# Time mix base rows loaded half a batch early into the sum's own tiles, modulation rows stored in two steps, gate floors on 128 partitions

## Chip, cores and metric

The kernel runs as one program on one core of a Trainium2 chip. The time is the device time of one execution in microseconds (us). The engines are named as in the profile: PE (TensorE), PEld (its weight loads), DVE (VectorE), ACT (ScalarE), POOL (GpSimd), SP (SyncE, which here only issues DMAs).

## What is computed

One AdaLN block on x of 4 batches x 512 tokens x 512 channels in float32. A small conditioning matrix c (4 x 512) gives six modulation rows per batch, `mod = (silu(c) @ wmod).reshape(4, 6, 1, 512)`: sa, ca, ga, sb, cb, gb. Two of them, ga and gb, are floored in size: `(2 * (g >= 0) - 1) * max(|g|, 0.25)`. Then:

```
h  = layernorm(x) * (1 + ca) + sa                       # h0 in the kernel
x2 = h + (sigmoid(r) * wkv) @ Wo.T                      # time mix; r, k, v from layernorm(h) and its shift by one token
x3 = x2 + sigmoid(...) * (silu(... @ Wkey.T) @ Wval.T)  # channel mix, from layernorm(x2)
x4 = x + ga * x3
h5 = layernorm(x4) * (1 + cb) + sb
out = x4 + gb * (shared experts(h5) + top-2 of 16 routed experts(h5))
```

The change touches four places: where h is added to the output projection of the time mix (x2), where the six modulation rows go to memory, where ga and gb are floored, and the element type of a small table of integers that the routed experts read.

## The kernel before, in words

The kernel is written by hand with one instruction stream for each engine, in a fixed order, and semaphores between them. Every float32 product is three matmuls of split operands (high x high, high x low, low x high; `mm3`, L423 to L427). There are three stages: the time mix (about the first 300 us), the channel mix (to about 690 us) and the experts.

**Time mix.** It runs over four batches b = 0 to 3, each of four tiles j of 128 tokens. For each batch PE computes K, V and R (48 matmuls each), turns the next batch's normalized rows over (L880), and then computes O, the output projection (48 matmuls, 12 for each tile), into the four banks `mm_ps[0]` to `mm_ps[3]`. The next user of bank j is K of the next batch. PE may start it only when DVE has read bank j (`bank_free`, which waits on `s_x2` after an O).

DVE reads the banks of O in `o_out(b, j)` (L1377 to L1386): `x2b[:, j] = mm_ps[j] + h0r[:, t % 2]`, where t = 4b + j. `h0r` is a ring of two tiles, into which SP loads the rows of h (`h0_s`) from memory (`load_h0`, L604 to L610). `h0_s` was stored by SP earlier (`store_h0`) from the tiles `xb`, because `xb` is overwritten with the next batch. The four calls of `o_out(b, .)` stand among the work on K and V of batch b + 1 in DVE's order (L1509 to L1533). Behind them come statistics of x2, and then first_norm_a to first_norm_d of batch b + 2 (L1446 to L1456), whose result is waited for by ACT, PE and POOL in turn: `centred(2, b)` gives ACT what it needs for `hn_out(2, b)`, and PE turns that over (`turn(2, b, ...)`) between V tile 1 and V tile 2 of batch b + 1, and between V tile 2 and V tile 3.

**SP's order in batch 0** (L638 to L673): store h of batch 0; store modulation rows 0 and 1; load the first norm's rows and x of batch 1; load four half weights (`load_tm` 4 to 7); wait for all six modulation rows (`s_modsb` at 7) and for the floors of ga and gb (`s_ke` at 3); store modulation rows 2 to 5; store h of batch 1; load half weights 8 and 9; wait until the six rows are in memory; load `h0r` for tiles 0 and 1; then the rows and x of batch 2; then, tile by tile, store x2 and load `h0r` for tile 2, and again for tile 3.

**Modulation rows.** ACT copies each row set (4 batches x 512) from PSUM to `modr` (4 partitions x 6 slots x 512; `rows_out`, L2086). The tile `modr` lies on the same memory as `h0r` (slots 0 and 1) and `x2b` (slots 2 to 5), so nothing may be loaded into these before the rows are stored. The rows come in the order 0, 1, 2, 5, 3, 4 (`row_order`, L401). DVE floors row 2 (ga) in `gate_floor(2)` at L1427, ahead of the first batch's differences, and row 5 (gb) in `gate_floor(5)` at L1501, between r_out and rw_lo of batch 0; each is four instructions on 4 partitions x 512. ga and gb are read from memory for the first time after the time mix.

**Table of words.** `tab` (1 x 2 x 52, int32) is written once by DVE (L1838). PE reads one word of it for each 128-row tile of the routed experts (`word_of`, L1178) and waits on a semaphore against it (`up`, L1189); SP reads two for each tile (`tile_of`, L818). There are 41 such tiles in this run.

Of the kernel before, what the change touches and what calls it, by code (L numbers as in the profile page):

```python
# [14 lines left out]
BF16 = mybir.dt.bfloat16  # L15
I32 = mybir.dt.int32
ALU = mybir.AluOpType
ACT = mybir.ActivationFunctionType
# [47 lines left out]
def adaln_block(nc, x_d, c_d, wmod_d, vecs_d, wtm_d, wcm_d, wrt_d, wex_d, out_d):  # L66
    top = ExitStack()
    with top:
# [27 lines left out]
        pos = sbuf(top, "pos", [P, 2, NT], I32)  # L96
        tab = sbuf(top, "tab", [1, 2, NSX], I32)
        tend = sbuf(top, "tend", [1, NE + 3], I32)
# [28 lines left out]
        overlay.close()  # L127
        h0r = sbuf(ph1, "h0r", [P, 2, H])
        x2b = sbuf(ph1, "x2b", [P, TT, H])
# [14 lines left out]
        sgc = sbuf(ph1, "sgc", [P, KT, NB])  # L144
        overlay = ExitStack()
        modt = sbuf(overlay, "modt", [NB, 2, H])
        overlay.close()
        srb = sbuf(ph1, "srb", [P, 2, H])
# [168 lines left out]
        s_srst = [sem("s_srst0"), sem("s_srst1")]  # L317
        s_h0r = [sem("s_h0r0"), sem("s_h0r1")]
        s_x2 = sem("s_x2")
# [80 lines left out]

        row_order = [0, 1, 2, 5, 3, 4]  # L401

        order1 = []
# [135 lines left out]
        def xk_in(b, k):  # L539

            n = b * KT + k
            if b:
                return xkr[:, n % 2], s_xkr[n % 2], 16 * (n // 2)
            if k < 2:
                return xkr[:, k], s_xkr[k], 16
            return raw[:, k - 2], s_h0r[k - 2], 16 * (NT // 2 + 1)

# [8 lines left out]
        def _(sp):  # L556
# [46 lines left out]

            def load_h0(b, tiles):  # L604
                for j in tiles:
                    t = b * TT + j
                    sp.wait_ge(s_h0st[j], 16 * (b + 1))
                    if t >= 2:
                        sp.wait_ge(s_x2, t - 1)
                    sp.dma_start(h0r[:, t % 2], h0_s[t]).then_inc(s_h0r[t % 2], 16)  # L610

# [27 lines left out]
            sp.wait_ge(s_modsb, 3)  # L639
            for i in (0, 1):  # L640
                sp.dma_start(mod_s[i], modr[:, i]).then_inc(s_modst, 16)
            load_bc(1)
            load_x(1)
            for n in (4, 5, 6, 7):
                load_tm(n)
            sp.wait_ge(s_modsb, 7)
            sp.wait_ge(s_ke, 3)
            for i in range(2, 6):
                sp.dma_start(mod_s[i], modr[:, i]).then_inc(s_modst, 16)
            for b in range(NB):  # L650
                if b + 1 < NB:
                    store_h0(b + 1)
                if b == 0:
                    load_tm(8)
                    load_tm(9)
                    sp.wait_ge(s_modst, 16 * 6)
                load_h0(b, [0, 1])
                if b + 2 < NB:
                    load_bc(b + 2)
                if b:  # L660
                    store_xk(b - 1)
                if b + 2 < NB:
                    load_x(b + 2)
                if b == NB - 1:
                    load_half(10, cm_half(10))
                    load_half(11, cm_half(11))
                if b:
                    store_sr(b - 1, [0] if b == NB - 1 else range(TT))
                store_x2(b, [0])
                load_h0(b, [2])  # L670
                store_x2(b, [1])
                load_h0(b, [3])
                store_x2(b, [2, 3])  # L673
            load_half(12, cm_half(12))
# [21 lines left out]
            sp.wait_ge(s_mm, mm_count("S", NB - 1, 3))  # L696
            sp.wait_ge(s_modst, 16 * 6)

# [559 lines left out]
        def _(dve):  # L1258
# [118 lines left out]
            def o_out(b, j):  # L1377
                if b == 0 and j == 0:
                    dve.wait_ge(s_modst, 16 * 6)
                t = b * TT + j  # L1380
                dve.wait_ge(s_mm, mm_count("O", b, j))
                dve.wait_ge(s_h0r[t % 2], 16 * (t // 2 + 1))
                if b:
                    dve.wait_ge(s_x2st[j], 16 * b)
                    dve.wait_ge(s_hn, hn_count(2, b - 1, j))
                dve.tensor_tensor(x2b[:, j], mm_ps[j][:, :], h0r[:, t % 2], ALU.add).then_inc(s_x2, 1)  # L1386

# [21 lines left out]

            def gate_floor(i):  # L1410

                src = modr[:, i]
                dve.wait_ge(s_modsb, row_count(i))
                done(dve.tensor_scalar(modt[:, 0], src, 0.0, 2.0, ALU.is_ge, ALU.mult))
                done(dve.tensor_scalar(modt[:, 1], src, -1.0, 0.25, ALU.mult, ALU.max))
                done(dve.tensor_tensor(modt[:, 1], src, modt[:, 1], ALU.max))
                dve.scalar_tensor_tensor(out=src, in0=modt[:, 0], scalar=-1.0, in1=modt[:, 1],
                                         op0=ALU.add, op1=ALU.mult).then_inc(s_ke, 1)
# [7 lines left out]
            dve.tensor_scalar(floor[:, :], vecs[:, V_FIRST, :], -1.0, PP0, ALU.mult, ALU.add).then_inc(s_ke, 1)  # L1426
            gate_floor(2)  # L1427
            differences(1, 0, [0, 1])
# [15 lines left out]
            for b in range(NB):  # L1444
# [34 lines left out]
                if b:  # L1479
                    mixed_lo("S", b - 1, 0)  # L1480
                    mixed("S", b - 1, 2)
                    mixed_lo("S", b - 1, 1)
                    mixed("X", b - 1, 0)
                    mixed("S", b - 1, 3)
                    mixed_lo("S", b - 1, 2)
                    r_out(b, 0)
                    mixed("X", b - 1, 1)
                    mixed_lo("S", b - 1, 3)
                    r_out(b, 1)
                    rw_lo(b, 0)  # L1490
                    mixed("X", b - 1, 2)
                    mixed("X", b - 1, 3)
                    r_out(b, 2)
                    rw_lo(b, 1)
                    r_out(b, 3)
                    rw_lo(b, 2)
                    rw_lo(b, 3)
                else:
                    r_out(b, 0)
                    r_out(b, 1)  # L1500
                    gate_floor(5)  # L1501
                    rw_lo(b, 0)
                    r_out(b, 2)
                    rw_lo(b, 1)
                    r_out(b, 3)
                    rw_lo(b, 2)
                    rw_lo(b, 3)
# [487 lines left out]
        def _(act):  # L1995
# [80 lines left out]
            def sr_out(b, tiles=range(TT)):  # L2076
                for j in tiles:
                    t = b * TT + j
                    act.wait_ge(s_mm, mm_count("S", b, j))
                    if t >= 2:  # L2080
                        act.wait_ge(s_srst[t % 2], 16 * (t // 2))
                    else:
                        act.wait_ge(s_ke, 3)
                    act.activation(srb[:, t % 2], mm_ps[j][:, :], ACT.Sigmoid).then_inc(s_sr, 1)

            def rows_out(i, bank):  # L2086

                act.wait_ge(s_modps, rows_summed(i))
                if i in (1, 4):
                    ins = act.activation(modr[:, i], bank[0:NB, :], ACT.Identity, bias=1.0)  # L2090
                else:
                    ins = act.activation(modr[:, i], bank[0:NB, :], ACT.Copy)
                ins.then_inc(s_modsb, 1)
# [530 lines left out]
```

## Time and profile before

| | |
|---|---|
| time, median of 3 runs | 942.76 us (938.45, 942.76, 944.33) |
| span of the profiled execution | 937.6 us from its first to its last instruction |
| busy share of the span | PE 95%, PEld 77%, DVE 56%, ACT 41%, POOL 41% |
| mean granted PE clock | 0.984 of full speed |
| chain of work that ended last | PE 71%, DVE 12%, DMA 5%, issue 4%, ACT 3%, POOL 3% |

The page gives no time of the profiled execution beside its span; the fastest of the three runs is 0.85 us above that span and the slowest 6.7 us. Times in the views count from the span's start. An engine's idle time is put down to what ended it ("<-"). Busy spans of PE overlap, as matmuls are pipelined: at full clock one 128x512 matmul starts 0.23 us after the one before and is shown as 0.39 us long.

### The profile page before, as it was taken

The numbers are of one execution on the slowest core, as the hardware profiler recorded it, in microseconds if no ns is written. First come the engines' busy times: TensorE is split into PE (matmuls) and PEld (weight loads), VectorE is DVE, ScalarE is ACT, GpSimd is POOL, SyncE is SP. The second block draws the span as 40 slices with busy tenths as digits, with TensorE's granted clock in tenths as the row PEclk, the third lists the DMA queues.
The fourth block names the chain that finished last, engine by engine and source line by source line (L and its number), as shares of the span: only waits on it lengthen the run. The fifth ranks groups of instructions, "written<-read, shape, count | busy, mean of one in ns | idle before, by whom it ended". The sixth has DMA issues, their size and how long they took to land.

```text
span 937.6 us, 13563 instructions
## 1 busy us (share of the span) xinstructions
PE 892.2 (95%) x4264; PEld 719.0 (77%) x4265; DVE 529.4 (56%) x999; ACT 383.2 (41%) x632; POOL 381.2 (41%) x282
## 2 busy tenths in 40 slices
PE   7899869999998999999999999999999999999996
PEld 2457658878776888788888888888877888888875
DVE  5897797988667111274327432742486444444488
ACT  2557565573736533322232223215452333333352
POOL 2332200100022446416301630167815599998573
PEclk9899989999998999999999999999999999999999
DMA  9548578566046426876212521267353789876887
GB/s 357 192 129 255 199 231 256 158 203 203 23 157 209 144 97 206 243 239 209 91 34 72 198 90 34 87 203 282 114 157 124 247 248 278 279 247 223 260 252 194
DMA packets 121824, 174.03 MB, mean 186 GB/s; under 512 B 8216, under 2 KB 69656, under 8 KB 118704
## 3 DMA queue, kind: packets, MB, share of 16 engines
q1 hardware_dynamic: 58896, 111.55, 34.9%
q0 software_dynamic: 9216, 34.61, 12.1%
q10 hardware_dynamic: 53664, 27.26, 9.9%
q8 instruction: 27, 0.44, 0.2%
q14 instruction: 21, 0.17, 0.1%
HBM read 97.58 MB, written 75.81 MB: 185 GB/s over the span
## 4 chain that ended last, share of the span: by engine, by line
PE 71%; DVE 12%; DMA 5%; issue 4%; ACT 3%; POOL 3%; SPq 1%; DVEq 0%; ACTq 0%
PE kk_ps L425 6%; PE kk_ps L427 6%; PE kk_ps L426 6%; PE kv_ps L425 6%; PE kv_ps L427 6%; PE kv_ps L426 6%; PE mm_ps L425 4%; PE mm_ps L426 4%; PE mm_ps L427 4%; PE up_ps L425 3%; PE dn_ps L425 3%; PE dn_ps L427 3%; PE dn_ps L426 3%; PE up_ps L426 2%; PE up_ps L427 2%
## 5 line engine op out<-in xcount | busy, mean ns | idle before, releaser
L1563 DVE TENSOR_TENSOR silu<-kk_ps,silu 128x512 fp32r<-128x512 f32 x64 | 44.2, 691 | 196.5 <-ACT silu L2229 196.2
L2225 ACT ACTIVATE kk_ps<-kk_ps 128x512 f32<-128x512 f32 x64 | 37.2, 582 | 206.5 <-PE kk_ps L427 206.5
L425 PE MATMUL kk_ps<-xk,cm_w 128*128 128x512 f32 x256 | 100.9, 394 | 2.3 <-DVE xk L1608 2.3
L425 PE MATMUL kv_ps<-cm_w,silu 128*128 128x512 f32 x256 | 100.6, 393 | 0.0
L427 PE MATMUL kk_ps<-xk,cm_w 128*128 128x512 f32 x256 | 99.8, 390 | 0.0
L427 PE MATMUL kv_ps<-cm_w,silu 128*128 128x512 f32 x256 | 99.7, 390 | 0.0
L426 PE MATMUL kk_ps<-xk,cm_w 128*128 128x512 f32 x256 | 99.6, 389 | 0.0
L426 PE MATMUL kv_ps<-cm_w,silu 128*128 128x512 f32 x256 | 99.6, 389 | 0.0
L2393 POOL TENSOR_TENSOR cm_w<-stage,cm_w 128x1024 fp32r<-128x1024 f32 x16 | 38.7, 2423 | 90.5 <-ACT cm_w L2013 74.7
L2400 POOL TENSOR_TENSOR rs<-mv,neghalf 128x4 f32<-128x4 f32 (+2 forms) x13 | 13.8, 1065 | 144.1 <-DVE mv L1274 144.0
L1890 DVE TENSOR_TENSOR xsT<-xs_ps,xsT 128x512 fp32r<-128x512 f32 x42 | 28.9, 691 | 73.9 <-ACT xsT L2310 73.9
L2449 POOL TENSOR_TENSOR rs<-mv,neghalf 128x1 f32<-128x1 f32 x16 | 16.1, 1008 | 126.9 <-DVE mv L1588 126.9
L2041 ACT ACTIVATE mix<-raw_ps 128x512 fp32r<-128x512 f32 x64 | 37.6, 596 | 66.8 <-DVE raw_ps L1345 63.5
L425 PE MATMUL mm_ps<-mix,wkv_w 128*128 128x512 f32 x128 | 54.0, 422 | 8.8 <-DVE x2b L1386 4.6
L425 PEld LDWEIGHTS kk_ps<-xk,cm_w 128*128 128x128 f32 x256 | 48.1, 188 | 12.1 <-ACT xk L2221 2.6
L427 PEld LDWEIGHTS kk_ps<-xk,cm_w 128*128 128x128 f32 x256 | 48.1, 188 | 10.3
L427 PEld LDWEIGHTS kv_ps<-cm_w,silu 128*128 128x128 f32 x256 | 48.0, 188 | 10.3
L426 PEld LDWEIGHTS kv_ps<-cm_w,silu 128*128 128x128 f32 x256 | 48.1, 188 | 9.8
L426 PEld LDWEIGHTS kk_ps<-xk,cm_w 128*128 128x128 f32 x256 | 48.1, 188 | 9.7
L425 PEld LDWEIGHTS kv_ps<-cm_w,silu 128*128 128x128 f32 x256 | 48.1, 188 | 9.6
L426 PE MATMUL mm_ps<-mix,wkv_w 128*128 128x512 f32 x128 | 52.3, 409 | 0.0
L2442 POOL DMA_INDIRECT xs_s<-stage,pos x32 | 31.5, 985 | 50.9 <-DVE pos L1682 42.4
(297 smaller groups left out, 2361.6 us busy)
## 6 DMA issues: line engine op xcount, KB each, us to landing
xs_s<-zero ACTq DMA_DIRECT2D x13, 1024.0 KB, 6.1
ys_s<-zero ACTq DMA_DIRECT2D x13, 1024.0 KB, 6.3
xsb<-xs_s SPq DMA_DIRECT2D x44, 256.0 KB, 3.8
ys_s<-ysb SPq DMA_DIRECT2D x41, 256.0 KB, 3.4
ex_raw<-in_wex POOLq DMA_DIRECT2D x9, 1024.0 KB, 6.3
stage<-in_wcm SPq DMA_DIRECT2D x16, 512.0 KB, 3.7
wmod<-in_wmod SPq DMA_DIRECT2D x6, 1024.0 KB, 11.8
ex_raw<-in_wex SPq DMA_DIRECT2D x6, 1024.0 KB, 8.0
```

The costliest lines, as they stand in the source:

```text
L425: pe.matmul(out, lhs[0], rhs[0], start=first, stop=False)
L426: pe.matmul(out, lhs[0], rhs[1], start=False, stop=False)
L427: return pe.matmul(out, lhs[1], rhs[0], start=False, stop=last)
L1563: dve.tensor_tensor(silu[:, g % NSILU, 1, :], kk_ps[g % 2][:, :], silu[:, g % NSILU, 0, :].bitcast(F32), ALU.subtract).then_inc(s_silo, 1)
L1890: dve.tensor_tensor(xsT[:, par, 1], xs_ps[par][:, :, :], xsT[:, par, 0].bitcast(F32), ALU.subtract)\
L2041: act.activation(mix[:, i % 2, 0, k, :], raw_at(s, b, k), ACT.Copy)\
L2225: act.activation(kk_ps[g % 2][:, :], kk_ps[g % 2][:, :], ACT.Silu).then_inc(s_silu, 1)
L2393: pool.tensor_tensor(w[:, 1, k0:k0 + KT // 2, :], stage[:, n % 2].rearrange("p (k c) -> p k c", c=H), w[:, 0, k0:k0 + KT // 2, :].bitcast( ...
L2400: pool.tensor_tensor(rs[:, j0:j1].rearrange("p (t a) -> p t a", a=1), mv[:, j0:j1, 1:2], neghalf[:, :].rearrange("p (t a) -> p t a", a=1). ...
L2442: pool.indirect_dma_start(xs_s, bass.IndirectOffsetOnAxis(ap=pos[:, c, t:t + 1], axis=0), h5_row(t), None).then_inc(s_scat[t % TT], 16)
L2449: pool.tensor_tensor(rs5[:, t % 2:t % 2 + 1], mv5[:, t % 2, 1:2], neghalf[:, :], ALU.pow)\
```

## The change

- `load_h0` loads all four tiles of a batch at once, straight into `x2b`, early in the batch's half; `o_out` adds the bank to `x2b` in place. The waits that guard `x2b` (its last store, and ACT's last reading) move from DVE's `o_out` to SP's `load_h0`. `h0r` is gone; in its room lie `flo` and a filler.
- The modulation rows get other slots (`row_slot`), so that rows 0 to 3 lie on `x2b`, and 4 and 5 on the room of `flo`. Rows 2 and 3 are stored when row 3 is there, without a floor; rows 4 and 5 later.
- `gate_floor(2)` and `gate_floor(5)` go. In their place SP loads ga and gb back from memory, spread over 128 partitions x 16 elements each, DVE floors both together in batch 1 (four instructions on 128 x 32), and SP stores them over the rows in memory.
- `tab` has 16-bit words.

```diff
-        tab = sbuf(top, "tab", [1, 2, NSX], I32)
+        tab = sbuf(top, "tab", [1, 2, NSX], U16)
...
-        h0r = sbuf(ph1, "h0r", [P, 2, H])
+        flo = sbuf(ph1, "flo", [P, 4, 2, H // 32])
+        sbuf(ph1, "flo_rest", [P, 2 * H - 4 * H // 16])
...
         row_order = [0, 1, 2, 5, 3, 4]
+        row_slot = [2, 3, 4, 5, 1, 0]
...
-            def load_h0(b, tiles):
-                for j in tiles:
-                    t = b * TT + j
+            def load_h0(b):
+                for j in range(TT):
                     sp.wait_ge(s_h0st[j], 16 * (b + 1))
-                    if t >= 2:
-                        sp.wait_ge(s_x2, t - 1)
-                    sp.dma_start(h0r[:, t % 2], h0_s[t]).then_inc(s_h0r[t % 2], 16)
+                    if b:
+                        sp.wait_ge(s_x2st[j], 16 * b)
+                        sp.wait_ge(s_hn, hn_count(2, b - 1, j))
+                    sp.dma_start(x2b[:, j], h0_s[b * TT + j]).then_inc(s_h0r[j], 16)
+
+            def store_rows(rows):
+                for i in rows:
+                    sp.dma_start(mod_s[i], modr[:, row_slot[i]]).then_inc(s_modst, 16)
+
+            def spread(i):
+                return mod_s[i].rearrange("b (q c) -> (b q) c", c=H // 32)
...
             for n in (4, 5, 6, 7):
                 load_tm(n)
-            sp.wait_ge(s_modsb, 7)
-            sp.wait_ge(s_ke, 3)
-            for i in range(2, 6):
-                sp.dma_start(mod_s[i], modr[:, i]).then_inc(s_modst, 16)
+            sp.wait_ge(s_modsb, row_count(3))
+            store_rows([2, 3])
             for b in range(NB):
                 if b + 1 < NB:
                     store_h0(b + 1)
                 if b == 0:
+                    sp.wait_ge(s_modst, 16 * 4)
+                load_h0(b)
+                if b == 0:
+                    sp.wait_ge(s_modsb, row_count(4))
+                    store_rows([4, 5])
                     load_tm(8)
                     load_tm(9)
-                    sp.wait_ge(s_modst, 16 * 6)
-                load_h0(b, [0, 1])
                 if b + 2 < NB:
                     load_bc(b + 2)
+                if b == 0:
+                    sp.wait_ge(s_modst, 16 * 6)
+                    for n, i in enumerate((2, 5)):
+                        sp.dma_start(flo[:, 0, n], spread(i)).then_inc(s_flo, 16)
                 if b:
                     store_xk(b - 1)
...
-                store_x2(b, [0])
-                load_h0(b, [2])
-                store_x2(b, [1])
-                load_h0(b, [3])
-                store_x2(b, [2, 3])
+                store_x2(b, range(TT))
+                if b == 1:
+                    sp.wait_ge(s_ke, 2)
+                    for n, i in enumerate((2, 5)):
+                        sp.dma_start(spread(i), flo[:, 3, n]).then_inc(s_modst, 16)
...
             def o_out(b, j):
-                if b == 0 and j == 0:
-                    dve.wait_ge(s_modst, 16 * 6)
-                t = b * TT + j
                 dve.wait_ge(s_mm, mm_count("O", b, j))
-                dve.wait_ge(s_h0r[t % 2], 16 * (t // 2 + 1))
-                if b:
-                    dve.wait_ge(s_x2st[j], 16 * b)
-                    dve.wait_ge(s_hn, hn_count(2, b - 1, j))
-                dve.tensor_tensor(x2b[:, j], mm_ps[j][:, :], h0r[:, t % 2], ALU.add).then_inc(s_x2, 1)
+                dve.wait_ge(s_h0r[j], 16 * (b + 1))
+                dve.tensor_tensor(x2b[:, j], mm_ps[j][:, :], x2b[:, j], ALU.add).then_inc(s_x2, 1)
...
-            def gate_floor(i):
+            def gate_floors():
-                src = modr[:, i]
-                dve.wait_ge(s_modsb, row_count(i))
-                done(dve.tensor_scalar(modt[:, 0], src, 0.0, 2.0, ALU.is_ge, ALU.mult))
...
+                src, sign, size, out = (flo[:, i].rearrange("p a c -> p (a c)") for i in range(4))
+                dve.wait_ge(s_flo, 32)
+                done(dve.tensor_scalar(sign, src, 0.0, 2.0, ALU.is_ge, ALU.mult))
+                done(dve.tensor_scalar(size, src, -1.0, 0.25, ALU.mult, ALU.max))
+                done(dve.tensor_tensor(size, src, size, ALU.max))
+                dve.scalar_tensor_tensor(out=out, in0=sign, scalar=-1.0, in1=size,
+                                         op0=ALU.add, op1=ALU.mult).then_inc(s_ke, 1)
...
-            gate_floor(2)
...
                     rw_lo(b, 3)
+                    if b == 1:
+                        gate_floors()
                 else:
                     r_out(b, 0)
                     r_out(b, 1)
-                    gate_floor(5)
...
-                    else:
-                        act.wait_ge(s_ke, 3)
                     act.activation(srb[:, t % 2], mm_ps[j][:, :], ACT.Sigmoid).then_inc(s_sr, 1)
```

## Rows read from the trace of the kernel before

**Rows 1.** Chain that ended last, 86 to 105 us: start, length, what.

```profile
86.64 8.48 DMA h0r<-h_s
95.24 0.70 DVE x2b L1386
...
96.78 6.89 DMA h0r<-h_s
```

**Rows 2.** Waits between 85 and 130 us: engine, line, releaser, total, times, longest.

```profile
PE tp_ps L880 <- ACT hT L2031: 7.0, 1, 7.0
...
DVE x2b L1386 <- DMA h0r<-h_s: 5.0, 2, 3.5
PE mm_ps L425 <- DVE x2b L1386: 4.6, 2, 2.8
```

**Rows 3.** Timeline of DVE, 93 to 113 us: start, length, instruction, idle before.

```profile
93.08 0.68 DVE L1351 TENSOR_TENSOR mix<-raw_ps,mix 128x512 fp32r<-128x512 f32 x1
95.24 0.69 DVE L1386 TENSOR_TENSOR x2b<-mm_ps,h0r 128x512 f32<-128x512 f32 x1 [1.47 <-DMA h0r<-h_s]
...
103.77 0.69 DVE L1386 TENSOR_TENSOR x2b<-mm_ps,h0r 128x512 f32<-128x512 f32 x1 [3.52 <-DMA h0r<-h_s]
...
112.54 0.16 DVE L1320 SCALAR_TENSOR_TENSOR nm<-mv,rs 128x4 f32<-128x4 f32 x1 [0.36 <-POOL rs L2400]
```

**Rows 4.** Timeline of PE, 93 to 129 us, in the same columns.

```profile
93.73 0.39 PE L427 MATMUL mm_ps<-wro_w,rw 128*128 128x512 f32 x1
95.99 0.50 PE L425 MATMUL mm_ps<-mix,wkv_w 128*128 128x512 f32 x1 [1.86 <-DVE x2b L1386]
...
104.51 0.50 PE L425 MATMUL mm_ps<-mix,wkv_w 128*128 128x512 f32 x1 [2.75 <-DVE x2b L1386]
...
105.32 0.52 PE L425 MATMUL mm_ps<-mix,wkv_w 128*128 128x512 f32 x1
...
108.96 0.40 PE L425 MATMUL mm_ps<-mix,wkv_w 128*128 128x512 f32 x1
...
117.49 1.09 PE L880 MATMUL tp_ps<-ident,hn 128*128 128x128 f32 x8 [0.16 <-ACT hn L2023]
...
128.29 1.94 PE L880 MATMUL tp_ps<-ident,hn 128*128 128x128 f32 x8 [6.96 <-ACT hT L2031]
```

**Rows 5.** Timeline of ACT, 59 to 117 us.

```profile
59.98 0.59 ACT L2092 ACTIVATE modr<-tp_ps 4x512 f32<-4x512 f32 x1 [1.88 <-PE tp_ps L863]
...
105.16 0.60 ACT L2041 ACTIVATE mix<-raw_ps 128x512 fp32r<-128x512 f32 x1 [5.48 <-DVE raw_ps L1345]
...
115.93 1.51 ACT L2023 ACTIVATE hn<-x2b,nm,rs 128x512 f32<-128x512 f32 x2
```

**Rows 6.** Waits of SP's queue, whole span.

```profile
SPq L647 <- DVE modr L1417: 27.0, 1, 27.0
...
SPq L575 <- DMA mod_s<-modr: 2.2, 1, 2.2
```

**Rows 7.** Timeline of DVE around the second floor, 80 to 83 us.

```profile
80.21 0.68 DVE L1417 SCALAR_TENSOR_TENSOR modr<-modt 4x512 f32<-4x512 f32 x1
...
82.79 0.69 DVE L1370 TENSOR_TENSOR eT<-mm_ps,eT 128x512 f32<-128x512 f32 x1
```

**Rows 8.** Timeline of DVE, batch 1, 149 to 161 us.

```profile
149.68 2.49 DVE L1327 TENSOR_TENSOR dT<-hT 128x512 f32<-128x512 f32 x4
...
160.52 0.69 DVE L1386 TENSOR_TENSOR x2b<-mm_ps,h0r 128x512 f32<-128x512 f32 x1 [1.87 <-PE mm_ps L427]
```

**Rows 9.** Groups of DVE by line and shape: count, busy, mean ns, idle before.

```profile
L1776 DVE TENSOR_TENSOR pr<-pr 128x32 f32<-128x32 f32 x1 | 0.2, 194 | 0.0
```

**Rows 10.** Busy time by stretch: PE, PEld, DVE, ACT, POOL, granted clock, DMA share, GB/s.

```profile
105.00:109.00 4.00, 4.00 (x13) 3.10 (x12) 3.90 (x11) 3.82 (x6) 2.22 (x1) 0.57 0.46 159
...
145.00:166.00 21.00, 21.00 (x103) 17.60 (x102) 17.43 (x27) 10.95 (x18) 0.00 (x0) 1.00 0.81 253
```

**Rows 11.** Waits between 660 and 860 us, the routed experts.

```profile
PEld up_ps L425 <- issue: 7.8, 33, 0.4
```

More of the change, by code:

```diff
@@ L16 @@
 I32 = mybir.dt.int32
+U16 = mybir.dt.uint16
 ALU = mybir.AluOpType
@@ L144, in adaln_block @@
         sgc = sbuf(ph1, "sgc", [P, KT, NB])
-        overlay = ExitStack()
-        modt = sbuf(overlay, "modt", [NB, 2, H])
-        overlay.close()
         srb = sbuf(ph1, "srb", [P, 2, H])
@@ L317, in adaln_block @@
         s_srst = [sem("s_srst0"), sem("s_srst1")]
-        s_h0r = [sem("s_h0r0"), sem("s_h0r1")]
+        s_h0r = [sem(f"s_h0r{i}") for i in range(TT)]
+        s_flo = sem("s_flo")
         s_x2 = sem("s_x2")
@@ L545, in xk_in @@
                 return xkr[:, k], s_xkr[k], 16
-            return raw[:, k - 2], s_h0r[k - 2], 16 * (NT // 2 + 1)
+            return raw[:, k - 2], s_h0r[k - 2], 16 * (NB + 1)
         def bank_free(eng, s, b, j):
@@ L639, in _ @@
             sp.wait_ge(s_modsb, 3)
-            for i in (0, 1):
-                sp.dma_start(mod_s[i], modr[:, i]).then_inc(s_modst, 16)
+            store_rows([0, 1])
             load_bc(1)
@@ L645, in _ @@
                 load_tm(n)
-            sp.wait_ge(s_modsb, 7)
-            sp.wait_ge(s_ke, 3)
-            for i in range(2, 6):
-                sp.dma_start(mod_s[i], modr[:, i]).then_inc(s_modst, 16)
+            sp.wait_ge(s_modsb, row_count(3))
+            store_rows([2, 3])
             for b in range(NB):
@@ L696, in _ @@
             sp.wait_ge(s_mm, mm_count("S", NB - 1, 3))
-            sp.wait_ge(s_modst, 16 * 6)
+            sp.wait_ge(s_modst, 16 * 8)
             def load_ga(b):
@@ L1408, in centred_last @@
                                          op0=ALU.mult, op1=ALU.mult).then_inc(s_nm3, 1)
-            def gate_floor(i):
-                src = modr[:, i]
-                dve.wait_ge(s_modsb, row_count(i))
-                done(dve.tensor_scalar(modt[:, 0], src, 0.0, 2.0, ALU.is_ge, ALU.mult))
-                done(dve.tensor_scalar(modt[:, 1], src, -1.0, 0.25, ALU.mult, ALU.max))
-                done(dve.tensor_tensor(modt[:, 1], src, modt[:, 1], ALU.max))
-                dve.scalar_tensor_tensor(out=src, in0=modt[:, 0], scalar=-1.0, in1=modt[:, 1],
+            def gate_floors():
[5 more added lines that the diff above has]
+                dve.scalar_tensor_tensor(out=out, in0=sign, scalar=-1.0, in1=size,
                                          op0=ALU.add, op1=ALU.mult).then_inc(s_ke, 1)
@@ L2088, in rows_out @@
                 act.wait_ge(s_modps, rows_summed(i))
+                row = modr[:, row_slot[i]]
                 if i in (1, 4):
-                    ins = act.activation(modr[:, i], bank[0:NB, :], ACT.Identity, bias=1.0)
+                    ins = act.activation(row, bank[0:NB, :], ACT.Identity, bias=1.0)
                 else:
-                    ins = act.activation(modr[:, i], bank[0:NB, :], ACT.Copy)
+                    ins = act.activation(row, bank[0:NB, :], ACT.Copy)
                 ins.then_inc(s_modsb, 1)
```

## The prediction, on record before the result

> **What bounds the kernel.** PE is busy for 95% of the span, so I looked first for the places where it is not, and for what stands behind them. The chain of waits shows one stretch in which a transfer ends last: two loads into `h0r`, 8.5 and 6.9 us, one ahead of the first `o_out` of batch 0 and one ahead of the third [rows 1]. The waits of the same stretch say who pays [rows 2]: DVE stood 5.0 us for the loads, and PE 4.6 us for DVE's reading of the banks. There is a second, longer gap of PE, 7.0 us for ACT's `hT`. Whether the change is worth 4.6 or 5.0 us, or less, hangs on what leads to that second gap.
>
> On DVE [rows 3] the work before the first `o_out` starts at 93.08 and ends at 93.76; then DVE idles 1.47 us for the first load. It idles 3.52 us for the load of tile 2 ahead of 103.77. Behind that it is all but continuous up to 112.54, where it waits 0.36 us for POOL. PE [rows 4] ends O of batch 0 at 93.73 + 0.39 = 94.12, starts K of batch 1 at 95.99, waits again ahead of 104.51, then for `hn` ahead of 117.49 (0.16 us), then for `hT` ahead of 128.29. The last two are waits for work that DVE's order leads to: statistics of x2, `hn_out`, first norm. So from 95 to 128 us DVE's order and PE's are both near the bound, and DVE's ends last at 117.49 and 128.29.
>
> **The change, part by part.**
>
> *Base rows.* The first load of `h0r` is issued at 86.64 [rows 1] because SP stands 27.0 us for all six rows and both floors [rows 6]. Afterwards SP waits only for row 3, which ACT has out at 59.98 + 0.59 = 60.6 [rows 5], and for four rows in memory: the nearest row for that wait is 2.2 us [rows 6]; doubled, 4.4 us, it still leaves SP free at 66. Four loads, with 1 us allowed for the issue of each and the longest landing, 8.5 us [rows 1], are in by 66 + 4 + 8.5 = 79 us. DVE can use them at 93.76, so there are about 15 us to spare. Both idle times go: 1.47 + 3.52 = 4.99 us on DVE. What is late next at each `o_out`? Tile 0 is then bound by DVE's own work (93.76), tile 2 too, at 103.77 - 4.99 = 98.78; its bank is ready at 94.12 at the latest.
>
> The rest of DVE's work up to 112.54 has one foreign term, POOL: it sits behind ACT's weight copies, which follow an ACT instruction that itself stood 5.48 us for DVE's `raw_ps` [rows 5]. So ACT and POOL move with DVE. The last `hn_out` (two instructions from 115.93, ending 117.44 [rows 5]) ends at 112.45.
>
> PE, seen alone, would gain more. K of batch 1 can start 0.06 us after the first `o_out`, which ends at 93.76 + 0.69 = 94.45, that is at 94.5 instead of 95.99: 1.48 us. The second gap, 2.75 us, goes, as bank 2 is read by 98.78 + 0.69 = 99.5 and PE reaches it at 94.5 + 24 x 0.23 = 100.0. And after that gap the granted clock was 0.57 for 4 us [rows 10]: nine matmul intervals took 108.96 - 105.32 = 3.64 us [rows 4] where nine of 0.2275 us take 2.05, so 1.6 us went to the lower of the two levels, 1.2 GHz. In all PE would come to its turn 1.48 + 2.75 + 1.6 = 5.8 us earlier, at 117.49 - 0.16 - 5.8 = 111.5. There it finds `hn` at 112.45 and waits 0.9 us. So the gain at this point is 4.99 us, and at the wait for `hT` too.
>
> Here a rule and the rows part. The Trainium skill (TensorE: Matmul & The Clock Gate, Part 1) says that the array runs throttled after idling and that activity releases it, which would price a removed gap at the gap and the slow stretch behind it. By that rule the sum is 5.8 us; by the rows it is 5.0, since DVE's order ends last. I take the rows.
>
> *Does it carry to the end?* From 130 us PE is busy without a break: in 145 to 166 us for 21.00 of 21.00 us [rows 10], and what follows waits on semaphores of these engines, not on a clock. No transfer of batch 1 to 3 is waited for by `o_out` (both waits for `h0r` [rows 2] lie in batch 0), so the early loads bring nothing there. They stand on SP behind two new waits, x2's last store and ACT's last reading; in batch 3, where the base loads come first in the turn, SP has then only stores queued behind. I cost that at nothing.
>
> *What SP is moved past.* Behind `load_h0` of batch 0 stand rows 4 and 5, half weights 8 and 9, the rows and x of batch 2. They come earlier than before, as the stop of 27.0 us is gone. The two loads and two stores of the floors on 128 partitions (64-byte pieces) add four issues, at the same allowance 4 us; nothing waits for their landing but DVE half a batch later. Cover: SP's idle time; without it 4 us on SP.
>
> *Floors.* The first floor ran while DVE waited for `hT`. The second ends at 80.89, its last and longest instruction 0.68 us long [rows 7], so all four take at most 2.7 us. But the last r_out at 82.79 waits for ACT's sigmoid, which stands in ACT's order behind the copies of what PE turns over, so taking that time away ahead of it moves nothing. The new floors are four instructions on 128 x 32, 0.19 us each by the nearest row [rows 9], 0.8 us with their waits, put ahead of 149.68 in batch 1 [rows 8]; DVE idles 1.87 us for PE ahead of 160.52, which hides it. Without that cover: 0.8 us.
>
> *16-bit words.* The trace shows no word load itself. The nearest row is PEld's "issue" ahead of `up` [rows 11]: 7.8 us in 33 times, 0.24 us for a tile, with the word's load and its waits in it. One word is read where one was read before, so I take 0. Bounds: the 0.24 us doubled for 41 tiles, +9.7 us; below, the 0.24 us gone, -9.7 us, which would need the load to be the whole gap and free afterwards, so I keep -1 at most for it.
>
> **Sum.** 4.99 us off, nothing added: the profiled execution's span goes from 937.6 to 932.6 us. The median of the runs shown, 942.76, stands 5.2 us above that span, the fastest 0.85 us; I carry the difference over: 942.76 - 4.99 = 937.8 us.
>
> **Rivals.**
>
> *PE's clock adds to it (0.13).* If the slow stretch behind 128.29 shrinks as well (eight turns in 1.94 us against 1.09 at 117.49 [rows 4], so 0.9 us, and about as much again in the matmuls behind it), the gain is 5.0 + 1.8 = 6.8: 936.0 us. For it: PE-bound from there. Against it: the 7 us gap ahead of it stays whole.
>
> *A new wait takes the place of the old one (0.12).* The change does then not do what it says: the base rows are still not there, or the turn finds something else late, such as the weights for S or x of batch 2. If only the first idle time goes, 942.76 - 1.47 = 941.3; if neither, 942.8. Against it: 15 us to spare, and loads behind it that are all moved forward. For it: the moved transfers meet the zero fills that ACT issues in 60 to 80 us.
>
> *The word load costs more (0.05): slower.* It is read on PE ahead of every routed tile's `up`, where PE has little slack. It decides from 4.99 / 41 = 0.12 us for each word on; at a doubled 0.24 us the time is 942.76 - 4.99 + 9.7 = 947.5. For it: PE's sequencer does stand there [rows 11]. Against it: the same instruction with a narrower operand.
>
> **Numbers.** The forecast has 0.70. Range: the runs shown spread from 938.45 to 944.33. Low end: 938.45 less 6.8 is 931.7. High end: the case of only the first wait, 941.3, with half of that spread, 1.5 to 3 us, is 943.5. I give 932 to 943.5; outside lie the word's case and single odd draws, under 0.2. A change of 1% here is 9.4 us (about what a measurement of this kernel tells from none): under 933.3 is faster, over 952.2 slower. The forecast of 0.53% lies within; the clock's case comes nearest to the one bound, the word's case reaches the other only at 0.35 us for each word. So faster 0.11, same 0.86, slower 0.03.
>
> **What would show it.** After the change DVE has no wait for a load at `o_out`, the first starts right behind the split ahead of it, and the third about 5 us after the first (8.5 before). PE's two waits for `x2b` in batch 0 shrink to some 0.4 us together, the clock stays at its upper level there, and PE waits about 1 us for `hn` ahead of the turn and still 7 us for `hT`. SP issues the base loads near 65 us. The floors show as four instructions of 0.2 us in batch 1 with PE's O unmoved. PEld's "issue" ahead of `up` stays at 0.24 us. The prediction is wrong if DVE's idle time reappears between 98 and 128 us, if batch 1's PE stretch starts less than 4.5 us earlier, or if the routed stage changes its length by more than 1 us.

## The result, and the profile after

The changed kernel takes 935.2 us (median of 9 runs), the kernel before 942.44 us (median of 9): a ratio of 0.9924, 95% interval 0.9899 to 0.9948, or 7.2 us less (4.9 to 9.5). One of the nine runs after took 1786.43 us; the ratio leaves it out. The forecast was 937.8 us and a ratio of 0.9947, just inside the interval. Two further sets of runs gave 0.9921 (0.9889 to 0.9954) and 0.9945 (0.9923 to 0.9967). The three, weighted by the inverse squares of their intervals, make 0.9933 (0.9918 to 0.9947), that is 6.3 us less (5.0 to 7.7). So there is a gain, and it is most likely a little more than the 5.0 us of the sum.

The profiled execution of the changed kernel spans 932.3 us, against 937.6. It reached batch 0's first `r_out` 0.68 us later than the one before (76.77 against 76.09). Over all 14 traces that mark lies between 75.63 and 77.20 us, and over the traces of each of the two orders it spreads by 0.75 us or more, so positions below are also given from it.

SP's timeline after, 61 to 85 us (start, length, instruction), answers to [rows 6] and to the loads of [rows 1]:

```profile
61.34 0.61 SPq L615 DMA_DIRECT2D mod_s<-modr  x2
61.98 1.80 SPq L603 DMA_DIRECT2D h_s<-xb  x4
63.88 2.22 SPq L611 DMA_DIRECT2D x2b<-h_s  x4
...
82.36 2.44 SPq L570 DMA_DIRECT2D xb<-in_x  x4
```

The stop of 27.0 us is gone, the four base loads are issued from 63.88, and batch 2's x, which left SP at 90.05 before, leaves at 82.36. DVE's timeline after, for [rows 3]:

```profile
93.83 0.68 DVE L1363 TENSOR_TENSOR mix<-raw_ps,mix 128x512 fp32r<-128x512 f32 x1
94.43 0.68 DVE L1392 TENSOR_TENSOR x2b<-mm_ps,x2b 128x512 f32<-128x512 f32 x1
...
99.34 0.67 DVE L1392 TENSOR_TENSOR x2b<-mm_ps,x2b 128x512 f32<-128x512 f32 x1
...
108.12 0.16 DVE L1332 SCALAR_TENSOR_TENSOR nm<-mv,rs 128x4 f32<-128x4 f32 x1 [0.35 <-POOL rs L2405]
```

Neither sum has an idle time in front of it. The first starts right behind the split; the third comes 4.91 us after the first, 8.53 before. POOL's 0.35 us stays. PE after, for [rows 4], with the restart in batch 2 as a last row:

```profile
95.17 0.50 PE L426 MATMUL mm_ps<-mix,wkv_w 128*128 128x512 f32 x1 [0.28 <-DVE x2b L1392]
...
113.06 1.09 PE L892 MATMUL tp_ps<-ident,hn 128*128 128x128 f32 x8 [1.27 <-ACT hn L2029]
...
123.88 1.94 PE L892 MATMUL tp_ps<-ident,hn 128*128 128x128 f32 x8 [6.98 <-ACT hT L2037]
...
185.23 1.30 PE L892 MATMUL tp_ps<-ident,hn 128*128 128x128 f32 x8 [1.12 <-ACT hT L2037]
```

PE's waits for `x2b` fell from 4.6 us [rows 2] to 0.28. It now comes to the turn early and waits 1.27 us for `hn`; the gap for `hT` is as long as before. Up to here the profile looks as forecast. The last row does not: the kernel before has 1.88 us at that place, not 1.12 (PE before):

```profile
190.47 1.76 PE L880 MATMUL tp_ps<-ident,hn 128*128 128x128 f32 x8 [1.88 <-ACT hT L2031]
```

The prediction had read nothing there; it had PE busy without a break from 130 us on, which it had read off the stretch from 145 to 166 us alone. The answer stands in three rows of DVE before that I had passed over (timeline of the kernel before, batches 1 and 2):

```profile
163.24 0.69 DVE L1386 TENSOR_TENSOR x2b<-mm_ps,h0r 128x512 f32<-128x512 f32 x1 [0.17 <-PE mm_ps L427]
166.72 0.69 DVE L1386 TENSOR_TENSOR x2b<-mm_ps,h0r 128x512 f32<-128x512 f32 x1 [0.92 <-PE mm_ps L427]
...
228.91 0.69 DVE L1386 TENSOR_TENSOR x2b<-mm_ps,h0r 128x512 f32<-128x512 f32 x1 [1.38 <-issue]
```

An O tile is 12 matmuls, 2.72 us, and the second sum of batch 1 follows the first ([rows 8], at 160.52) by just that. The third follows the second by 3.48 us. Its idle time is put down to PE, and that of the third sum of batch 2, at 228.91, to "issue", which names nothing. But the load for the third sum of batch 1 was issued at 161.66 and took 5.0 us:

```profile
L610 SPq DMA_DIRECT2D h0r<-h_s x1: 1179/1179/1179, 161.7 to 161.7; - x1
...
DMA to landing us min/median/max: 5.0/5.0/5.0
```

161.7 + 5.0 is 166.7, where the sum starts. In batch 2 the load was issued at 223.41 and took 5.4 us, which gives 228.8. In the changed kernel the same sums come evenly:

```profile
158.75 0.69 DVE L1392 TENSOR_TENSOR x2b<-mm_ps,x2b 128x512 f32<-128x512 f32 x1 [0.17 <-PE mm_ps L428]
161.47 0.69 DVE L1392 TENSOR_TENSOR x2b<-mm_ps,x2b 128x512 f32<-128x512 f32 x1 [0.17 <-PE mm_ps L428]
```

And behind the gap of 1.88 us the kernel before ran a stretch of PE at its lower level. The busy time by stretch shows the granted clock in the third column from the end, before:

```profile
190.50:194.50 4.00, 4.00 (x15) 3.26 (x16) 3.97 (x7) 3.09 (x5) 0.00 (x0) 0.57 0.96 283
```

and the same four microseconds behind the gap after:

```profile
185.30:189.30 4.00, 3.96 (x21) 3.26 (x22) 3.96 (x7) 3.07 (x5) 0.00 (x0) 1.00 1.06 306
```

### The profile page after: what moved, and what is told of

It is laid out like the page before. It is cut to its first block, busy times and chain, and to the rows that moved or that the text cites. A ratio compares the mean times of both kernels' runs of the same rounds, so it can differ in the third digit from the quotient of the medians.

```text
span 932.3 us, 13546 instructions
## 1 busy us (share of the span) xinstructions
PE 890.4 (96%) x4264; PEld 717.8 (77%) x4265; DVE 525.8 (56%) x995; ACT 382.9 (41%) x632; POOL 380.5 (41%) x282
## 3 DMA queue, kind: packets, MB, share of 16 engines
q10 hardware_dynamic: 53664, 27.26, 10.3%
## 4 chain that ended last, share of the span: by engine, by line
PE 80%; DVE 8%; DMA 4%; issue 3%; ACT 2%; POOL 2%; DVEq 0%; SPq 0%; ACTq 0%
PE kk_ps L426 6%; PE kk_ps L428 6%; PE kk_ps L427 6%; PE kv_ps L426 6%; PE kv_ps L428 6%; PE kv_ps L427 6%; PE mm_ps L426 6%; PE mm_ps L428 6%; PE mm_ps L427 6%; PE up_ps L426 4%; PE dn_ps L426 3%; PE dn_ps L428 3%; PE dn_ps L427 3%; PE up_ps L427 3%; PE up_ps L428 3%
## 5 line engine op out<-in xcount | busy, mean ns | idle before, releaser
L426 PE MATMUL mm_ps<-mix,wkv_w 128*128 128x512 f32 x128 | 53.0, 414 | 3.9 <-DVE mix L1363 3.1
L1357 DVE SCALAR_TENSOR_TENSOR raw_ps<-dT,vecs,hT 128x512 f32<-128x512 f32 x64 | 50.2, 801 | 3.0
```

Of the source, the lines that this page charges most:

```text
L426: pe.matmul(out, lhs[0], rhs[0], start=first, stop=False)
L1357: dve.scalar_tensor_tensor(out=out, in0=dT[:, k, :], scalar=vecs[:, vec, k:k + 1], in1=hT[:, k, 0:T], op0=ALU.mult, op1=ALU.add).then_inc( ...
```

## The experiments

**The theory.** All of the gain comes from loads of base rows that DVE no longer waits for: two in batch 0, as forecast, and one in batch 1, as just read. **Rivals.** The floors carry part of it; the 16-bit words, or the 192 bytes by which they move later tiles, carry part; the excess over 5.0 us is chance.

Each kernel was timed in five rounds beside the kernel before, and profiled once. There were three such sets, on three chips; the kernel before had medians of 940.82, 941.78 and 940.97 us in them. The ratios are not quotients of these medians: floors only, for one, has 938.14 against 940.82 us, a quotient of 0.997, and a ratio of 0.9995. The changed kernel ran in the first and the third set, not in the one with the late tiles. From the last sum of the time mix to the end the 14 traces lie between 656.4 and 665.2 us, in no order of the kernels, and that spread is more than the parts in question. So the parts are read inside the time mix, from batch 0's first `r_out`. "Gap" is PE's wait for `hT` in batch 2, and "behind it" the time from its end to batch 2's first sum; all in us, worked out from the timelines of DVE and PE.

| kernel | ratio (95%) | mark to first sum | first to third | b = 1, second to third | gap | behind it | mark to last sum |
|---|---|---|---|---|---|---|---|
| before | 1 | 19.15 | 8.53 | 3.48 | 1.88 | 31.80 | 204.37 |
| 16-bit words | 0.9995 (0.9968 to 1.0023) | 18.39 | 8.87 | 2.99 | 1.42 | 30.37 | 202.42 |
| the same again | 0.9996 (0.9970 to 1.0022) | 19.01 | 8.63 | 2.91 | 1.32 | 30.38 | 203.07 |
| floors only | 0.9995 (0.9971 to 1.0020) | 17.46 | 6.62 | 3.52 | 1.92 | 31.96 | 201.52 |
| 2, 3 late, all | 0.9934 (0.9910 to 0.9957) | 17.68 | 5.52 | 3.59 | 1.99 | 31.97 | 200.57 |
| 2, 3 late, b = 1 to 3 | 0.9941 (0.9914 to 0.9967) | 17.58 | 4.91 | 3.32 | 1.73 | 30.38 | 197.25 |
| 2, 3 late, b = 0 | 0.9917 (0.9885 to 0.9950) | 18.02 | 5.47 | 2.72 | 1.12 | 30.37 | 197.32 |
| SP late | 0.9949 (0.9928 to 0.9970) | 17.97 | 4.91 | 2.72 | 1.12 | 30.39 | 197.05 |
| base only | 0.9916 (0.9885 to 0.9948) | 17.41 | 4.90 | 2.72 | 1.16 | 30.37 | 196.54 |
| changed | 0.9924 (0.9899 to 0.9948) | 17.66 | 4.91 | 2.72 | 1.12 | 30.37 | 197.00 |
| changed again | 0.9921 (0.9889 to 0.9954) | 17.56 | 4.90 | 2.73 | 1.12 | 30.36 | 197.07 |
| changed, third | 0.9945 (0.9923 to 0.9967) | 17.63 | 4.91 | 2.72 | 1.15 | 30.37 | 196.70 |

The order before has three traces (the first three lines), mean 203.29; the changed kernel three, mean 196.92. The difference, 6.4 us, agrees with the 6.3 us of the ratios. For the other kernels a row is a single trace, and the order before spreads by 2 us over its three, so a part below that is no more than what one trace shows.

**The changed kernel again.** No edit.

> The changed kernel once more, as the measure for the parts. Theory (the late base rows carry the gain): 0.990 to 0.995 of before, some 7 us less; in the profile no wait for a load at `o_out` in any batch, O's sums 2.7 us apart in batches 1 and 2. Rival (part of the 7 us was the luck of single executions): nearer to the 5.0 us of my sum, 0.9947.

Measured: 932.73 us, 0.9921, sums 2.7 us apart in both batches. The same kernel in a later set:

> The changed kernel a third time, for the size of the gain and as the measure beside the others of this set. My sum: 0.9947 of before. With the waits of batches 1 and 2 and the slow-clock stretch of batch 2 in it: 0.992 to 0.993.

Measured: 935.52 us, 0.9945, which is my sum's figure, while its trace has the shortest time mix of the three. One set's ratio does not tell 5.0 from 7 us; the time mix of the three traces, 196.70 to 197.07 us, is narrower.

**16-bit words alone.**

```diff
-        tab = sbuf(top, "tab", [1, 2, NSX], I32)
+        tab = sbuf(top, "tab", [1, 2, NSX], U16)
```

> Only the table's words are changed to 16 bits (all later tiles of on-chip memory move by 192 bytes). Theory: 1.000 of before within 0.15%, PEld's issue ahead of `up` still 0.24 us for a tile. Rival (the words or the moved addresses carry the 2 us that my sum lacks): 0.998 or less, with the gain in the routed stage for the words, anywhere for the addresses.

Measured: 940.43 us, no difference. The waits of this kernel in the routed stage have for [rows 11]:

```profile
PEld up_ps L426 <- issue: 8.0, 34, 0.4
```

8.0 / 34 is 0.24 us for a tile, as before. The rival of words or addresses falls. The second trace:

> The kernel before with 16-bit words once more, as a second trace of the order before. Theory: the third sums of batches 1 and 2 wait for their loads again (some 0.3 to 1 us and 1.2 to 1.8 us), and the stretch of batch 2 behind PE's gap for hT runs long (31.8 us up to the first sum) where that gap is 1.9 us or more, short (30.4 us) where it is below 1.75. Time: 1.000 of before within 0.2%.

Measured: 939.23 us. The third sums wait again (2.91 against 2.72 in batch 1, 4.28 in batch 2), with a short stretch behind a short gap. So this kernel shows the order before, without the fall of the clock in batch 2.

**Base rows alone**: the changed kernel with the floors as before.

```diff
+            gate_floor(2)
             differences(1, 0, [0, 1])
...
+            sp.wait_ge(s_ke, 2)
             store_rows([2, 3])
...
+                    gate_floor(5)
                     rw_lo(b, 0)
...
-                    if b == 1:
-                        gate_floors()
```

> The changed kernel with the floors as before: on 4 partitions, at their old places in DVE's order, rows 2 and 3 stored only after the first floor, rows 4 and 5 after the second and behind the loads of x. Base rows still early into the sum's tiles. Theory: all of the gain, 0.990 to 0.995 of before and within 1 us of the changed kernel; both 128-partition floors and the two-step store without a floor are worth nothing on the path. Rival (the floors' 2.2 us of DVE lie on the path): 2 us slower than the changed kernel.

Measured: 932.63 us, 0.9916, and a time mix of 196.54 us. All the gain is there with the floors at their old places, so the rival that the floors carry part of it falls: the second floor ran in time that DVE otherwise spends waiting for ACT's sigmoid. In the changed kernel, whose floor is gone, that wait is what is found in its place (DVE's timeline after):

```profile
83.53 0.69 DVE L1382 TENSOR_TENSOR eT<-mm_ps,eT 128x512 f32<-128x512 f32 x1 [2.36 <-ACT mm_ps L2074]
```

**Floors alone**: before, with 16-bit words, floors on 128 partitions in batch 1, and the ring kept.

```diff
-            sp.wait_ge(s_ke, 3)
             for i in range(2, 6):
                 sp.dma_start(mod_s[i], modr[:, i]).then_inc(s_modst, 16)
...
-            gate_floor(2)
-                    gate_floor(5)
+                    if b == 1:
+                        gate_floors()
```

> The kernel before with 16-bit words and only the floors moved: on 128 partitions in batch 1, rows 2 to 5 stored unfloored in one go when the last is out; the ring of two base tiles is kept and tiles 2 and 3 are still loaded behind x2's stores. Theory: SP comes to the first base loads earlier, so the first wait (1.47 us) goes, the second (3.5 us in batch 0) and those of batches 1 and 2 stay: 0.998 of before, 1.5 us less (1 to 2.5). Rival (floors carry part of the gain themselves): 3 us or more less. Rival (the first wait's place is taken by another): no change.

Measured: 938.14 us, 0.9995 (0.9971 to 1.0020); by its ratio it cannot be told from the kernel before, nor from the expected 0.998. The time mix is 203.29 - 201.52 = 1.8 us shorter, near the 1.5 expected, but not in the way expected. The first wait is gone, and the second has shrunk too, which I had said would stay:

```profile
93.65 0.68 DVE L1396 TENSOR_TENSOR x2b<-mm_ps,h0r 128x512 f32<-128x512 f32 x1
...
100.27 0.69 DVE L1396 TENSOR_TENSOR x2b<-mm_ps,h0r 128x512 f32<-128x512 f32 x1 [1.63 <-DMA h0r<-h_s]
```

Batch 0 gains 1.4 + 2.1 us; 1.7 us are lost again behind the third sum, with a gap of 1.92 us and a long stretch behind it.

**Tiles 2 and 3 late again**, in all batches, in batch 0 alone, and in the others alone (`early` stands for false, `b`, and `b == 0`).

```diff
-                load_h0(b)
+                load_h0(b, range(TT) if early else [0, 1])
...
-                store_x2(b, range(TT))
+                if early:
+                    store_x2(b, range(TT))
+                else:
+                    store_x2(b, [0])
+                    load_h0(b, [2])
+                    store_x2(b, [1])
+                    load_h0(b, [3])
+                    store_x2(b, [2, 3])
```

> The changed kernel, but SP loads the base rows of tiles 2 and 3 of every batch where it did before, behind x2's stores of tiles 0 and 1; tiles 0 and 1 early, all into the sum's own tiles. Theory (the later waits carry the gain, in batches 1 and 2 too): 3.5 us of the wait in batch 0 come back, 0.75 and 1.2 us at the third sum of batches 1 and 2, and a low-clock stretch with them: 4 to 6 us slower than the changed kernel, 0.997 to 0.999 of before. Rival (what counts is one free tile more, not the time of the load): within 1 us of the changed kernel.

> As the one before, in batch 0 alone: tiles 2 and 3 late there, early in batches 1 to 3. My prediction's sum: 3.5 us slower than the changed kernel (5.1 with PE's clock), so 0.996 to 0.998 of before. If the waits of batches 1 and 2 also count, this kernel keeps 0.7 to 3 us of gain beside the 1.5 us of the first wait.

> The opposite: tiles 2 and 3 early in batch 0, late in batches 1 to 3. Prediction as recorded (no transfer of batches 1 to 3 is waited for): the same as the changed kernel within 0.5 us. New theory (the third sum of batches 1 and 2 waited for its load, 0.75 and 1.2 us, and the delay made PE's gap for hT in batch 2 longer, with a slow-clock stretch behind it): 1 to 2.5 us slower than the changed kernel, the third sum of batch 1 some 3.5 us behind the second again.

Measured: 936.35, 934.93 and 936.5 us, ratios of 0.9934, 0.9917 and 0.9941. In all three I was wrong about the size of a part. The times do not tell these kernels from the changed one. For all batches late I had expected 0.997 to 0.999, which lies outside the interval (0.9910 to 0.9957); its time mix is 3.65 us longer than the changed kernel's, but that is one trace, and the longest of its ten executions (942.57 us). What follows is therefore read from the traces. In batch 0 the late loads cost 0.6 us, not 3.5 (DVE of the kernel with batch 0 late):

```profile
99.72 0.69 DVE L1399 TENSOR_TENSOR x2b<-mm_ps,x2b 128x512 f32<-128x512 f32 x1 [0.48 <-DMA x2b<-h_s]
```

The loads were issued at 95.72 and 97.79, where SP before issued them at 96.78 and 98.84, but now they landed in 3.6 to 3.9 us (6.5 to 6.9 before):

```profile
L611 SPq DMA_DIRECT2D x2b<-h_s x2: 456/630/804, 95.7 to 97.8; - x2
...
DMA to landing us min/median/max: 3.6/3.8/3.9
```

In this kernel SP had issued x of batch 2 from 81.76, before from 90.05. With the floors alone moved it was 85.80, and the first of these two loads took 5.0 us, in between. So the wait of 3.52 us was mostly a slow load, and the load was slow where x was asked for late, which came of the one stop of 27.0 us. That the x transfers themselves slowed it fits all three and is not shown apart from the rest. In batches 1 and 2 the load's wait now has its name in the profile (DVE with all batches late):

```profile
162.37 0.69 DVE L1399 TENSOR_TENSOR x2b<-mm_ps,x2b 128x512 f32<-128x512 f32 x1 [1.04 <-DMA x2b<-h_s]
...
224.75 0.69 DVE L1399 TENSOR_TENSOR x2b<-mm_ps,x2b 128x512 f32<-128x512 f32 x1 [1.38 <-DMA x2b<-h_s]
```

and batch 1's comes out at PE's gap in batch 2, with the clock at the lower level behind it (eight turns in 1.75 us):

```profile
186.13 1.75 PE L899 MATMUL tp_ps<-ident,hn 128*128 128x128 f32 x8 [1.99 <-ACT hT L2044]
```

The rival of one free tile more falls with these rows: all four base tiles are free here, and the third sums are as late as before (3.59 and 3.93 us behind the second; 3.48 and 3.92 before). The table makes the rest a rule of this kernel. What the third sum of batch 1 is late by (its distance less 2.72: 0.76, 0.27, 0.19, 0.80, 0.87, 0.60) is what the gap is longer by (less 1.13: 0.75, 0.29, 0.19, 0.79, 0.86, 0.60), in all six traces with late loads. In the three with a gap of 1.88 us and more the way behind it took 1.4 to 1.6 us longer; in the other nine, up to 1.73 us, it did not. So the kernel with late loads in batches 1 to 3 lost only 0.3 us (197.25 against 196.92), where I had expected 1 to 2.5: its clock did not fall. Batch 2's late sum (3.9 to 4.3 us) costs nothing: from batch 2's first sum to batch 3's it is 50.0 us before (222.27 to 272.30) and after (215.60 to 265.62).

**SP late**: base only, but rows 2 to 5 stored together after both floors, and the four base loads behind half weights 8 and 9, as before.

```diff
-            sp.wait_ge(s_modsb, row_count(3))
-            sp.wait_ge(s_ke, 2)
-            store_rows([2, 3])
+            sp.wait_ge(s_modsb, 7)
+            sp.wait_ge(s_ke, 3)
+            store_rows([2, 3, 4, 5])
```

> The base rows of all four tiles are loaded in one go into the sum's tiles, but as late as in the kernel before: the floors are on 4 partitions at their old places, and SP stores rows 2 to 5 together only when both floors are done, then loads half weights 8 and 9, then the base rows. Theory (two separate delays: SP's stop made the first load late; tiles 2 and 3 asked for only behind x2's stores met the x loads of the same burst): the first sum waits 0.5 to 2 us for its load again, the third and those of batches 1 to 3 don't; 1 to 2 us slower than the changed kernel, 0.993 to 0.995 of before. Rival (SP's earlier burst alone is what counts): 3 us or more slower than the changed kernel, with a wait at the third sum as well.

Measured: 935.07 us, 0.9949; a time mix of 197.05 us. The first wait that I expected is not there (DVE):

```profile
95.17 0.68 DVE L1385 TENSOR_TENSOR x2b<-mm_ps,x2b 128x512 f32<-128x512 f32 x1
```

The loads were issued from 87.11 and took 7.5 to 7.9 us; the first, with 7.9, was in by 95.0 us, just ahead of the 95.17. Each half of the edit in SP brings the 5.0 us of batch 0 by itself, to within 1 us: SP free early (tiles 2 and 3 late in batch 0), or all four tiles asked for at once. From the mark to the third sum these two have 23.49 and 22.88 us, the changed kernel 22.53 and the order before 27.53. The rival that SP's earlier burst alone counts falls.

**Tile 3 of V ahead of the turn's second half**, in the changed kernel, for the gap of 7 us that the change leaves.

```diff
                 channels_out("V", b, [2])
-                if b:
-                    turn(2, b - 1, [2, 3])
-                else:
+                if b == 0:
                     modulation(4, tp_ps[1][:, :, :].rearrange("p j c -> p (j c)"))
                 channels_out("V", b, [3])
+                if b:
+                    turn(2, b - 1, [2, 3])
```

> The changed kernel with one move on PE: in batches 1 to 3 tile 3 of V is computed ahead of the second half of the turn of x2's normalized rows, not behind it. PE stands 7.0 us for hT there in batch 1, 1.1 in batch 2, 0.6 in batch 3, and tile 3 of V is 12 matmuls, 2.7 us, which wait for nothing of this. Theory (PE's wait for hT is the late event, the turn's end does not become later): 2.7 us less in batch 1 and 1 to 1.7 us in the others, 3 to 4.5 us faster than the changed kernel, 0.988 of before. Rival (what follows waits for the turn in turn, on DVE's differences ahead of R): the gap moves in front of R and nothing is gained; or PE's later turn costs up to 1.5 us in batches 2 and 3.

> The order with tile 3 of V ahead of the second half of the turn, once more and beside the changed kernel on one chip. Theory: 2 to 4 us faster than the changed kernel, 0.987 to 0.990 of before; PE's gap for hT in batch 1 is 4.2 us, 7.0 without the move.

Measured: 930.59 us, 0.9872 (0.9843 to 0.9901), and 932.5 us, 0.9917 (0.9885 to 0.9949), the second beside 935.52 us of the changed kernel. The time mix is 195.14 and 193.13 us, 1.8 and 3.8 us less. PE of the first trace:

```profile
122.45 1.94 PE L892 MATMUL tp_ps<-ident,hn 128*128 128x128 f32 x8 [4.25 <-ACT hT L2037]
...
182.76 1.29 PE L892 MATMUL tp_ps<-ident,hn 128*128 128x128 f32 x8 [0.68 <-ACT hT L2037]
...
257.94 0.50 PE L426 MATMUL mm_ps<-wro_w,rw 128*128 128x512 f32 x1 [2.23 <-ACT srb L2088]
```

The gap shrinks by the 2.7 us of the 12 matmuls (4.27 us are left in the second trace). 1.5 us come back in batch 3 as a longer wait for `srb`, in both traces (2.23 and 2.27 us, 0.69 in the changed kernel). The order has the lowest median of both sets in which it ran. Its lead over the changed kernel, 3.0 us on one chip, lies inside the width of the intervals, and the second ratio misses the expected 0.987 to 0.990.

## Why the prediction was right, and where it was wrong

**The base rows in batch 0: right.** From the mark to the third sum the three traces before have 27.53 us on average (18.85 + 8.68), those after 22.53 (17.62 + 4.91): 5.00 us, against 4.99. That the two agree so closely is in part luck: the first wait of the three traces was 1.47, 0.56 and 1.41 us and the second 3.52, 3.86 and 3.63, so the same sum from the other two traces would have been 4.42 and 5.04. The prediction gave as a sign of its being wrong that PE's stretch in batch 1 starts less than 4.5 us earlier. From the mark it starts 5.09 us earlier (52.20 to 47.11); on the clock of the two executions only 4.41 (128.29 to 123.88), as the mark itself came 0.68 us later.

**Rows against rule.** I had priced PE alone at 5.8 us, the gaps and the slow stretch behind the second, and taken the 5.0 of DVE's order. From the mark PE reached its wait ahead of the turn 6.2 us earlier, and then stood 1.27 us for `hn` (forecast 0.9); the turn began 5.1 us earlier (41.40 to 36.29). The Trainium skill (TensorE: Matmul & The Clock Gate, Part 1) has the array throttled after idling. The trace before agrees with it (2.75 us idle, then a clock of 0.57); in the first trace with 16-bit words no slow stretch followed, as PE idled 3.13 us at that place and kept its clock:

```profile
103.86 0.50 PE L426 MATMUL mm_ps<-mix,wkv_w 128*128 128x512 f32 x1 [3.13 <-DVE x2b L1387]
```

Its busy time by stretch, for [rows 10]:

```profile
105.00:109.00 4.00, 3.96 (x18) 2.95 (x17) 3.90 (x11) 3.98 (x6) 2.87 (x2) 1.00 0.35 121
```

It has 1.00 where [rows 10] has 0.57, and yet its turn came at 40.96 us from the mark (41.40 before), with 1.45 us of waiting for `hn` where [rows 4] has 0.16. The 0.4 us between the two are those of DVE's third sum (27.26 and 27.68 us from the mark). The slow stretch at 105 to 109 us was free: what PE gained without it, it waited away.

**The failed step: "No transfer of batch 1 to 3 is waited for by `o_out`", and "From 130 us PE is busy without a break".** I had trusted the waits by name, which put both of `h0r`'s into batch 0. In batches 1 and 2 the third sum also ended its wait on the load. Batch 1's lateness reached PE in batch 2. Behind the third sum of batch 0 the traces before need 175.76 us to the last sum on average, those after 174.40: 1.36 us that the sum lacked. Of these 0.41 are the gap (1.54 against 1.13) and 0.48 the stretch behind it (30.85 against 30.37, the clock having fallen in one trace of three). The other 0.47 lie between the 7 us gap and batch 1's first sum, 32.23, 32.63 and 32.93 before against 32.15, 32.34 and 31.89, where only the length of the slow stretch differs from trace to trace. That these belong to the change is not shown: two kernels that are alike in batch 0 (tiles 2 and 3 late in all batches, and in batch 0 alone) have 32.61 and 31.55 there. So 5.9 of the 6.4 us are accounted for, 0.5 of them by a fall of the clock that one trace in three had.

**SP's moves: right.** The base loads left at 63.88 (forecast near 65) and landed in 3.3 to 4.1 us, half of the 8.5 allowed. What I did not see is that the second load was long in the order that SP's stop brought, and short in one without the stop.

**Floors: right at nothing.** In batch 1 they are four instructions (DVE after, first and last):

```profile
145.70 0.18 DVE L1420 TENSOR_SCALAR flo<-flo 128x32 f32<-128x32 f32 x1
...
146.36 0.19 DVE L1423 SCALAR_TENSOR_TENSOR flo<-flo 128x32 f32<-128x32 f32 x1
```

From start to end 0.85 us (forecast 0.8), and DVE's idle time ahead of batch 1's first sum covered it (0.59 us left, 1.12 and 1.13 in the other two traces; 1.89 in the kernel without them there).

**16-bit words: right at nothing** (two ratios of 0.9995 and 0.9996). In the changed kernel PEld's issue ahead of `up` is 8.3 us in 37 times, 0.22 us each.

**The rivals.** The clock's rival asked for the right kind of gain in the wrong place: the turn behind the 7 us gap is still 1.94 us long, and it was the stretch in batch 2 that shrank. No new wait took the old one's place in full: `hn` took 1.3 of the 6.2 us that PE came earlier, and the rest arrived. The routed stage, whose length I had made a test to 1 us, differs more than that between executions of one kernel (from its first `up` to its last 151.6, 155.9 and 154.4 us in the three traces of the changed kernel), so it tested nothing.

## What to carry over

Where an instruction waits for several semaphores, the wait's name in the profile can hide a load: look at the spacing of the repeated instructions, and at issue plus landing of the load, in every round of the loop and not only where a transfer is named. A late load can have a cause upstream, as here a queue's stop moved the issue of other loads close to it; freeing the queue and asking earlier were then two cures for one fault, whose gains did not add. And when a gap on the busiest engine goes, the sum should say which other order ends last behind it, as here DVE's did.

## What was not expected of the hardware

- A gap did not always bring the lower clock. Ahead of the restart at 104 us PE idled 2.75 us and then had a granted clock of 0.57 for 4 us, but in the kernel with 16-bit words it idled 3.13 us there and kept 1.00. Behind the 7 us gap matmuls started 0.43 us apart in every trace that has it, but that pace ended 3.0 to 5.9 us behind the restart, and 3.8, 4.3 and 4.7 us behind it in the three traces of the changed kernel.
- A 256 KB load issued at the same place in the order took 6.5 to 6.9 us where x's four loads had been issued 4 to 9 us ahead of it, and 3.6 to 3.9 us where that was 11 to 16 us. With 8 to 11 us between them, in the kernel with the floors alone moved, it took 4.7 to 5.0 us.
- Executions of one kernel differed in the later stages as well: from the last sum of the time mix to the end the three traces of the changed kernel have 658.5, 665.2 and 657.6 us, those of the order before 657.1, 661.2 and 658.6. A change of 5 us is read from the stage that it touches, not from one span.
